# Products with the row of maxima moved to the end of a step, on four 32-row tiles of TensorE

## The reference

```
xn   = group_norm(x, 32 groups)
q, k, v = Wq xn, Wk xn, Wv xn              # per batch: 768 x 1024
for each batch and head (64 x 1024 each):
    scores = q^T k / 8                     # 1024 x 1024
    attn   = softmax(scores, over the keys)
    out    = v attn^T
y = x + Wp out
```

## Time and profile before

| what | value |
|---|---|
| median of 3 runs | 3598.19 us (3596.39 to 3599.04) |
| time of the profiled execution | 3599.69 us |
| its span, first to last instruction | 3597.9 us |
| mean granted TensorE clock | 0.981 |
| busy: PE, PE weight load | 3451.4 us (96%), 2374.1 us (66%) |
| busy: VectorE, ScalarE, GpSimd | 1429.2 us, 1116.7 us, 1846.7 us |

### The profile page before, as it was taken

One profiled execution on the slowest core, in us unless ns is written; L12 is line 12 of the kernel. 1 busy time (PEld: TensorE's weight loads), 2 busy tenths in 40 slices (PEclk: granted clock), 3 DMA queues, 4 the chain that ended last, 5 costly groups with the idle time before them and its releaser, 6 DMA issues.

```text
span 3597.9 us, 51581 instructions
## 1 busy us (share of the span) xinstructions
PE 3451.4 (96%) x18656; PEld 2374.1 (66%) x18656; DVE 1429.2 (40%) x1739; ACT 1116.7 (31%) x1992; POOL 1846.7 (51%) x795
## 2 busy tenths in 40 slices
PE   6999999999999899999999999999999999999999
PEld 5888888888888655555555555555555555555556
DVE  5333323333232255544444444444444444444431
ACT  3111111111111044533433434334343343433431
POOL 3000000000000089977878768778777777877873
PEclk9999999999999899999999999999999999999999
DMA  6233342333422423334343343443343434334324
GB/s 214 103 132 111 141 145 102 131 111 141 144 102 101 163 85 116 127 127 141 118 145 128 106 152 119 140 146 108 124 142 127 144 119 130 130 118 153 115 92 170
DMA packets 259123, 464.45 MB, mean 129 GB/s; under 512 B 60640, under 2 KB 109920, under 8 KB 257632
## 3 DMA queue, kind: packets, MB, share of 16 engines
q1 hardware_dynamic: 258912, 461.67, 37.3%
HBM read 260.11 MB, written 200.67 MB: 128 GB/s over the span
## 4 chain that ended last, share of the span: by engine, by line
PE 58%; DMA 4%; issue 1%; DVE 1%; SPq 1%; ACT 0%; POOL 0%; DVEq 0%; ACTq 0%; POOLq 0%
PE psum L751 20%; PE psum L764 18%; PE psum L783 9%; PE psum L734 8%; DMA a<-o_parts 2%; PE psum L845 1%; DMA o_parts<-o_lo 1%; PE psum L774 1%; DVE half_max L924 1%; SPq L564 0%; DMA q<-o_parts 0%; ACT p_all L877 0%; SPq L612 0%; DMA k<-k_parts 0%; POOL sums L707 0%
## 5 line engine op out<-in xcount | busy, mean ns | idle before, releaser
L707 POOL TENSOR_TENSOR sums<-sums,p_all 128x1024 f32<-128x1024 f32 x576 | 1352.8, 2384 | 95.3 <-ACT p_all L877 95.1
L924 DVE TENSOR_REDUCE half_max<-psum 128x2 f32<-128x1024 f32 x768 | 939.5, 1225 | 753.5 <-PE psum L734 728.1
L877 ACT ACTIVATE p_all<-psum 128x512 f32<-128x512 f32 x1536 | 793.6, 602 | 1076.8 <-PE psum L751 1074.0
L764 PE MATMUL psum<-p_all,v 128*64 128x512 f32 x3072 | 744.1, 605 | 0.0
L751 PE MATMUL psum<-q,k 64*128 64x512 f32 x4608 | 674.4, 397 | 2.0 <-ACT p_all L877 0.3
L715 POOL TENSOR_TENSOR wp<-sums,wp 128x1536 fp32r<-128x1536 f32 x1 | 3.5, 3466 | 1177.8 <-ACT wp L910 1177.8
L751 PEld LDWEIGHTS psum<-q,k 64*128 64x128 f32 x4608 | 440.2, 190 | 110.3 <-ACT p_all L877 29.8
L783 PE MATMUL psum<-a,wp 128*128 128x512 f32 x1512 | 393.3, 414 | 74.2 <-DMA a<-o_parts 74.2
L734 PEld LDWEIGHTS psum<-k,q 64*128 64x128 f32 x1536 | 243.2, 312 | 319.6 <-DVE half_max L924 199.0
L240 PE MATMUL psum<-xn_hi,w_hi 128*128 128x512 f32 x1128 | 440.8, 391 | 6.9 <-DVE stage L377 6.9
L240 PE MATMUL psum<-xn_hi,w_lo 128*128 128x512 f32 x1128 | 440.0, 390 | 0.0
(11 more groups left out here) (72 smaller groups left out, 2500.7 us busy)
## 6 DMA issues: line engine op xcount, KB each, us to landing
q_parts<-stage SPq DMA_DIRECT2D x192, 256.0 KB, 2.2
k_parts<-stage SPq DMA_DIRECT2D x192, 256.0 KB, 2.3
q<-q_parts SPq DMA_DIRECT2D x48, 1024.0 KB, 6.7
k<-k_parts SPq DMA_DIRECT2D x48, 1024.0 KB, 8.8
a<-o_parts SPq DMA_DIRECT2D x84, 512.0 KB, 6.1
v_rows<-stage SPq DMA_DIRECT2D x128, 192.0 KB, 2.1
v<-v_rows SPq DMA_DIRECT2D x48, 512.0 KB, 3.9
recip_all<-recip_rows SPq DMA_DIRECT2D x96, 256.0 KB, 3.9
```

Source lines behind the costliest of these rows:

```text
L707: pool.tensor_tensor(sums[:, m % 2, i, :], first, p_all[:, i, n, :], ALU.add).then_inc(added, 1)
L764: mm = pe.matmul(heads[part, h, :], v[:, e, t, part], p_all[:, i, (m * MT + t) % EXPS, cols], start=(t == 0), stop=(t == MT - 1))
L877: act.activation(p_all[:, i, (m * MT + t) % EXPS, h * BANK:(h + 1) * BANK], psum[:, SCORE_BANKS[2 * h + i], :], ACT.Exp, scale=SCALE).then ...
L924: dve.tensor_reduce(half_max[:, :, t, h], of, AX.X, ALU.max, negate=True).then_inc(max_done, 1)
```

## The change

The product with `top` is taken out of `scores_by_key` and put in a function `lower`, which runs once in a step, behind both halves. Its four matmuls (two heads, two halves) have 32 rows each, on rows 0, 32, 64 and 96 of the array, and write the same four banks as before; `s_ready` is raised by these four. `top` now has the maxima of head i and half h in row (2 * i + h) * 32 and is half as wide, so the SP queue fills it with four copies in place of two, and the counts of `top_in` are 64 in place of 32 for a pair. The wait for `top_in` moves from ahead of the first half to ahead of `lower`.

```diff
-        top = sb("top", [P, SLOTS, N], F32R)
+        top = sb("top", [P, SLOTS, BANK], F32R)
...
                 for i in range(2):
-                    sp.dma_start(f32(top[i * DH:i * DH + 1, m % SLOTS, :]).rearrange("a (p t) -> a p t", t=MT),
-                                 f32(neg_max[:, m % 2, i, :])).then_inc(top_in, 16)
+                    for h in range(2):
+                        r = (2 * i + h) * QUARTER
+                        sp.dma_start(f32(top[r:r + 1, m % SLOTS, :]).rearrange("a (p t) -> a p t", t=MT),
+                                     f32(neg_max[half_of[h], m % 2, i, :])).then_inc(top_in, 16)
...
             def scores_by_key(p, m, t, h):
                 e = m % SLOTS
-                if t == 0 and h == 0:
-                    pe.wait_ge(top_in, 32 * (p + 1))
...
-                for c in range(4):
+                for c in range(3):
                     for i, part in enumerate(half_of):
                         left, right = ((k[part, e, 0, keys], q[part, e, 0, cols]), (k[part, e, 0, keys], q[part, e, 1, cols]),
-                                       (k[part, e, 1, keys], q[part, e, 0, cols]), (ones_r[part, :], top[part, e, cols]))[c]
-                        mm = pe.matmul(psum[:, SCORE_BANKS[2 * h + i], :], left, right, start=(c == 0), stop=(c == 3))
-                        if c == 3:
-                            mm.then_inc(s_ready, 1)
+                                       (k[part, e, 1, keys], q[part, e, 0, cols]))[c]
+                        pe.matmul(psum[:, SCORE_BANKS[2 * h + i], :], left, right, start=(c == 0), stop=False)
+
+            def lower(p, m, t):
+                e = m % SLOTS
+                if t == 0:
+                    pe.wait_ge(top_in, 64 * (p + 1))
+                for h in range(2):
+                    for i in range(2):
+                        quarter = slice((2 * i + h) * QUARTER, (2 * i + h + 1) * QUARTER)
+                        pe.matmul(psum[:, SCORE_BANKS[2 * h + i], :], ones_r[quarter, :], top[quarter, e, :],
+                                  start=False, stop=True, tile_position=((2 * i + h) * QUARTER, 0)).then_inc(s_ready, 1)
...
                     scores_by_key(p, m, t, 0)
                     scores_by_key(p, m, t, 1)
+                    lower(p, m, t)
                     maxima(late)
```

More of the change, by code:

```diff
@@ L928, in join @@
                 dve.wait_ge(max_done, (p + 1) * UNITS)
-                wait(dve, top_in, 32 * (p - 1))
+                wait(dve, top_in, 64 * (p - 1))
                 dve.tensor_reduce(neg_max[:, m % 2, :, :], half_max[:], AX.X, ALU.min).then_inc(neg_done, 1)
```

## The result

3767.4 us as the median of 4 runs (3766.6 to 3768.8), against 3597.3 us for the kernel before beside them: 1.047 times as long, 95% interval 1.046 to 1.049. That is +170 us; the forecast was +189 and its own range 3745 to 3835. The profiled execution has a span of 3767.0 us. In the kernel after, L734, L764, L783, L877, L924, L930 and L564 have become L736, L772, L791, L886, L933, L939 and L566, and the product with `top` is L760; in the experiments lines are shifted by a few more.

A forecast was written before the change was run, and what follows sets the result against it. TensorE, busy 96% of the span, was taken as the bound. 47 pairs at 3.68 us gave 173 us, plus 16 from SP, 189 in all: 3787 us, 5.3% slower, range 3700 to 3880 (own range 3745 to 3835).

The forecast's parts named there:

- The price of a change of shape: Plain step: changes into and out of the 32-row tiles make 0.82 us in place of 0.46, +0.36 us a step.
- the gap of 0.12: TensorE at each change of tile shape: 0.12 us more than a slot of 0.23 us.
- The visible part of a plain load: TensorE after a change of shape: a 128-column weight load no longer hidden, 0.12 us.
- The prediction's last paragraph: Signs expected in the profile after, such as loads starting with their matmuls and a plain step of about 4.89 us.
- Steps 0 and 1: First two steps of a head pair: exponentials start after `lower`, +1.52 us together, 0.80 of it new wait for ScalarE.
- The SP queue: Two more copies a pair, 1.17 us, ahead of the stores in 14 stalls of TensorE for `a`: 16 us.
- Covers: Other waits stay hidden: over 3 us of TensorE work against 0.43 + 2.07 of ScalarE; VectorE's reduction lies beside `values`.
- the change of shape is free: Rival: no price between 64 and 32 rows, a plain step loses 0.23 us; 3581 us, −0.5%; chance 9%.
- The gap alone: Rival: 0.12 us stop at each change, weights loaded meanwhile; plain step +0.01 us; 3666 us; chance 7%.
- two and two: Rival: the four 32-row matmuls need two slots, 88 us on top, 3875 us; chance 8%, most of it there.

The follow-up runs named there:

- The order alone: Kernel before with the products with `top` moved to the end of the step, still on two 64-row halves with two copies: 3646.7 us, 1.013.

## Why the prediction was right

**The price of a change of shape.** The mechanism held: loads at both changes start with their matmuls, two per step are added, and doubling them (3942 us) and keeping 64 rows (3647 us) went as worked out. The Trainium skill (TensorEngine Tiling, Key Properties) says that a change of mode drains TensorE; the trace agrees for 64 to 32 rows and back, with about 0.10 us from the end of the last slot to the next load. The step was mis-sized: +0.36 us forecast, +0.28 measured. From the last score pair to the 32-row load it is 0.33 (0.35 forecast), from there to the load of L736 0.43 (0.47), from there to L772's 0.55 (0.58). I took the gap of 0.12 three times from one place, the 0.35 us from L734 to L764 in the earlier trace rows; the median of these 369 changes in the trace before is 0.33, a gap of 0.10, and the gap after is the same. The visible part of a plain load was 0.12 in one place of the earlier trace rows and is 0.10 here. 47 x 6 x 0.08 = 23 us too much, more than the whole error. (The prediction's last paragraph puts the load of L736 0.35 us behind the 32-row matmuls; its own sum has 0.47.)

**Steps 0 and 1.** +1.52 forecast, +1.42 measured: 5 us too much. The order alone was to give 0.95 a pair, 46 us, and gave 48. With two copies in either kernel and the queue out of the way the change costs 147.5 us, so some 100 us are left for the shape of the tiles.

**The SP queue.** 16 us forecast; 15 in the kernel before with four copies, 26 in the kernel after, of which 20.5 are waiting. The term was too small by up to 10 us, which hid part of the other two errors: that the total came within 20 us is in part luck. That the stall comes from copies in front of the store is shown by the runs that moved the store; that four copies would be free behind it was not run.

**Covers.** GpSimd is in no wait of TensorE from 1300 to 3660 us, and the copies make it wait once, for 0.7 us: next to nothing, as said. That VectorE's reduction still lies beside other work was right for this order, but I did not say by how little in the other orders.

**The rivals.** That the change of shape is free is refuted, and its price was worked out wrongly: it counted the whole saved slot of 0.23 us. With both slots gone the late unit waits for VectorE, and a plain step gains 0.16 (4.37 by the timeline of that run), not 0.46. A rival that frees one slot can gain no more a step than freeing both. With 0.16 in place of 0.23 it would have been 0.69 − 6 x 0.16 = −0.27 a pair, −13 + 16 = +3 us: no gain even with free changes. That is worked out, not run. The gap alone is refuted by the loads that start with their matmuls; two and two by the four starts in one slot.

## What to carry to other kernels

Matmuls that use less of the array side by side save slots only among others of the same tile shape: read in the timeline whether the load at each change starts ahead of its matmul, and charge the gap and the visible load for the way in and the way out, the longer load above all. Before counting a freed slot as gained, ask which wait it covered; here a reduction was done less than 0.2 us before the load that waited for it. And where a queue carries both a copy that waits for a late result and a store that others wait for, the store goes first: that was worth 1.9%, and 2.4% with the loads ahead too, more than the 1.6% that leaving the product out altogether gave.

## What was not expected of the hardware

Two 32-row matmuls between two changes of shape cost as much as four (0.42 and 0.43 us from load to load), and four loads as much as two (0.19 and 0.18 us). Removing about 5 us of stall in 14 places gave back 87 us, while the recorded wait was 74: the granted clock over the span went from 0.981 to 0.992. In the kernel after it fell to 0.50 in the stall that ends at 2037.28, while the array stood idle, and was still there for the first 2.92 us of matmuls behind it; from 2036 to 2048 it is 0.75 on average, against 1.00 in a plain stretch:

```profile
2037.28:2040.20 2.92, 2.92 (x8) 1.69 (x8) 0.00 (x0) 0.00 (x0) 0.00 (x0) 0.50 1.04 419
2036.00:2048.00 12.00, 10.09 (x48) 5.88 (x50) 3.64 (x4) 3.17 (x7) 0.00 (x0) 0.75 0.78 298
2100.00:2110.00 10.00, 10.00 (x64) 5.02 (x62) 5.38 (x6) 4.34 (x9) 8.73 (x5) 1.00 0.08 19
```

Such a wait costs more than its length, because the matmuls behind it run at the lower of the two clocks (1.2 of 2.4 GHz) for a while.
